# Cross attention: the maxima of two PSUM banks taken by one VectorE instruction, four banks for maxima and two for scores

## The chip, the cores and the metric

One core of one Trainium2 chip runs the whole program. The metric is device microseconds of one execution; lower is better. The kernel before was timed in three runs, and one more execution was taken with the hardware profiler.

## The reference

The kernel computes one decoder layer over x of 8 batches x 256 rows x 128 features: a causal self attention, a cross attention, and a rotary attention with 31 routed experts. The change is in the cross attention alone, for each batch b:

```
q = layernorm(x) @ Wq + bq                   # 256 x 128: 16 heads of 8 features
k, v = split(ctx_768 @ Wkv + bkv)            # 1601 x 128 each, contraction over 96
attn = softmax(q k^T / sqrt(8))              # per head 256 queries x 1601 keys, no mask
x = x + (attn v) @ Wo + bo
```

The softmax has to take off each query's largest score before the exponential.

## The kernel before, in words

Five engines run their own instruction streams and meet at semaphores. The program is a sequence of blocks: self attention, cross attention (`cross_attention`, about 300 to 1090 us of the profile, its main part from 350 us on), rotary attention, gates and experts. Within the cross attention:

- **Operands.** Queries and keys are split in three bf16 parts, whose six products are stacked along the partitions (`q_stack`, `k_stack`, 48 of 64 rows of a half), so that one bf16 matmul gives an accurate fp32 score. SyncE bounces the parts through DRAM scratch tensors (`bounce`, L976) and reads them back stacked (`load_half`, L989; half 0 serves heads 0 to 7, half 1 heads 8 to 15).
- **Groups.** The 16 heads make 4 groups of `GH` = 4. `part(i, r, ...)` works on the 13 key tiles (`KT`) of group g = (r + 1) % 4, one **step** n per key tile. So a batch is 4 parts of 13 steps. The last part of a batch, group 0, is already the next batch's.
- **Scores of a step** (L1387). Two halves (`par` 0 and 1) of two heads each: 2 matmuls of 256 queries into one PSUM bank, then ScalarE takes the exponential of the 128x512 half (L1277) into `b_prob`. The halves rotate over three banks, (5, 6, 7).
- **Values** (`values`, L1351). Four fp32 matmuls (eight instructions in the profile) of `b_prob` with `b_v_aug`, each in its own 32 columns of the array, summed over 13 steps in bank 1. Those of step n - 1 are issued in step n, behind the scores of step n.
- **Maxima.** Before a group is started its 256x1601 scores have to be known once for their maxima. A **unit** (`unit`, L1342) is one matmul of 128 queries of one head against a quarter of the keys (`CHUNKS`, 400 or 401 columns), for which VectorE takes one maximum per row (L1142) into `b_chunk_max`. A group has `UNITS_B` = 2 x 4 x 4 = 32 units; they rotate over three banks, (2, 3, 4). `units_of_step` spreads them over the steps of the part before: steps 0 to 8 (`M_STEP` = 9) do the last 21 (`HEAD`) units of the next group, steps 9 to 12 the first 11 of the one after it, 2 or 3 in a step. After a group's last unit VectorE folds `b_chunk_max` into `b_mneg` (L1146).
- **Items** (`PREP_AT`, L823, and `item`). At most one in a step, all through bank 0 (`prep`), each waiting until the one before is out of it (`prep_free`). Per batch: four `k` (keys of the next batch: two fp32 matmuls on PE, L1304; two ScalarE copies, L1230 and L1231; a split on GpSimd), `x`, `q`, four `v`, four `m` (transposes of `b_mneg`, L1324, which become the shift rows of `q_stack` by four small DMAs, L999), four `pv` (normalisation of a group, L1329 and L1160 to L1161 on VectorE), `attnT` and `out`. `("k", 0)` stands at r = 0, n = 0, the other `k` at n = 3, 5, 7, `pv` at n = 2 of each part, `m` at n = 9 of each, `q` at r = 0, n = 11. At r = 0, n = 2 VectorE also scales the next batch's rows (`norm_scale`, L127), in front of that step's units.
- **Waits of PE.** Score half i waits for exponential i - 3 (three banks), unit v for maximum v - 3, the values of a step for that step's second exponential. The first unit of a half (r = 1 and r = 3, n = 9) waits for the reload of that half (`stacked`).

The order of a step on PE (`part`, L1373) is: both score halves; the first unit; the second; the item; the values of the step before; the third unit where there is one. The prologue takes all 32 maxima of group 0 and 11 of group 1 before the first step. In the last batch nothing is prepared for a next one, and from r = 1, n = 9 on there are no units either.

## Time and profile before

| | |
|---|---|
| median of 3 runs | 1765.2 us (1760.3 to 1766.73) |
| the profiled execution, its own time | 1764.87 us |
| its span in the profile | 1763.0 us |
| busy over the span | PE 1537.7, DVE 1124.7, ACT 918.5, POOL 557.0 us |
| granted TensorE clock, mean | 0.939 of 2.4 GHz |

A tile name is the program's without buffer numbers; L1142 is a line of the kernel before. PE is TensorE's matmul stream, PEld its weight loads, DVE VectorE, ACT ScalarE, POOL GpSimd, SPq the DMA queue of SyncE. A timeline row has the start (us from the span's start), the length, the engine, the line, the operation, how many instructions were merged in it, and in brackets how long the engine sat idle before it and what ended that. Matmuls overlap: their ends are modelled, and what a matmul costs its engine is the distance from its start to the next one's.

### The profile page before, as it was taken

The numbers are of one execution on the slowest core, as the hardware profiler recorded it, in microseconds if no ns is written. First come the engines' busy times: TensorE is split into PE (matmuls) and PEld (weight loads), VectorE is DVE, ScalarE is ACT, GpSimd is POOL, SyncE is SP. The second block draws the span as 40 slices with busy tenths as digits, with TensorE's granted clock in tenths as the row PEclk, the third lists the DMA queues.
The fourth block names the chain that finished last, engine by engine and source line by source line (L and its number), as shares of the span: only waits on it lengthen the run. The fifth ranks groups of instructions, "written<-read, shape, count | busy, mean of one in ns | idle before, by whom it ended". The sixth has DMA issues, their size and how long they took to land. (4 is left out here: it accounts for less than half of the span.)

```text
span 1763.0 us, 29632 instructions
## 1 busy us (share of the span) xinstructions
PE 1537.7 (87%) x10917; PEld 836.1 (47%) x10941; DVE 1124.7 (64%) x2537; ACT 918.5 (52%) x1996; POOL 557.0 (32%) x690
## 2 busy tenths in 40 slices
PE   1677686699999999999999997899999997599998
PEld 1344343244454544444444443666666675244443
DVE  4755443587878786878787882566665663355554
ACT  1223233076777767777767775455555553234333
POOL 4010102030211212030303000788887884133332
PEclk9988787599999999999999998999999997699999
DMA  4222211703232323232332300000000000000001
GB/s 103 68 56 55 55 37 42 132 19 81 48 99 48 99 48 99 48 99 48 91 56 72 55 7 9 1 1 2 1 1 1 1 1 1 10 20 20 23 20 36
DMA packets 76276, 75.32 MB, mean 43 GB/s; under 512 B 11813, under 2 KB 65477, under 8 KB 75205
## 3 DMA queue, kind: packets, MB, share of 16 engines
q1 hardware_dynamic: 76132, 73.44, 18.9%
q8 instruction: 87, 1.43, 0.3%
q14 instruction: 57, 0.46, 0.1%
HBM read 42.73 MB, written 30.42 MB: 41 GB/s over the span
## 5 line engine op out<-in xcount | busy, mean ns | idle before, releaser
L1142 DVE TENSOR_REDUCE b_chunk_max<-psum 128x1 f32<-128x400 f32 (+1 forms) x1024 | 540.5, 570 | 161.6 <-PE psum L1348 154.5
L1277 ACT ACTIVATE b_prob<-psum 128x512 f32<-128x512 f32 (+1 forms) x832 | 450.5, 594 | 182.1 <-PE psum L1387 176.2
L1348 PE MATMUL psum<-k_stack,q_stack 128*128 128x400 bf16 (+1 forms) x1024 | 286.5, 343 | 21.0 <-DMA k_stack<-b_k_scratch 16.8
L1357 PE MATMUL psum<-b_prob,b_v_aug 128*32 128x256 f32 (+1 forms) x3328 | 265.8, 391 | 1.7 <-ACT b_prob L1277 0.4
L1387 PE MATMUL psum<-q_stack,k_stack 128*128 128x256 bf16 (+1 forms) x1664 | 254.2, 275 | 3.7 <-ACT b_prob L1277 3.3
L1387 PEld LDWEIGHTS psum<-q_stack,k_stack 128*128 128x128 bf16 (+1 forms) x1664 | 145.6, 99 | 123.1 <-ACT b_prob L1277 74.6
L2025 DVE TENSOR_TENSOR e_hg<-e_gl,e_gate 128x512 f32<-128x512 f32 x128 | 125.0, 996 | 113.0 <-PE psum L2040 65.9
L1546 POOL TENSOR_SCALAR c_prob<-c_prob,c_rec 128x128 f32<-128x128 f32 (+1 forms) x256 | 192.5, 769 | 8.9 <-POOL c_kT L1555 8.3
L1629 DVE SCALAR_TENSOR_TENSOR c_turned<-psum,c_bias,c_tab 128x256 f32<-128x256 f32 x256 | 106.1, 476 | 111.9 <-PE psum L1762 111.9
L1664 ACT ACTIVATE c_prob<-psum,c_mneg 128x128 f32<-128x128 f32 (+1 forms) x256 | 104.3, 419 | 136.2 <-DVE c_mneg L1606 136.2
L1348 PEld LDWEIGHTS psum<-k_stack,q_stack 128*128 128x128 bf16 x1024 | 99.6, 98 | 131.9 <-DVE b_chunk_max L1142 97.4
L2006 ACT ACTIVATE e_gl<-psum,b1T 128x512 f32<-128x512 f32 x128 | 87.9, 687 | 140.9 <-PE psum L2053 134.7
L2040 PE MATMUL psum<-e_hg,e_w 128*128 128x512 f32 x256 | 132.3, 600 | 8.9 <-DVE e_hg L2025 8.9
L2053 PE MATMUL psum<-anT,e_w 128*128 128x512 f32 x256 | 133.5, 605 | 1.4 <-PEq L1811 1.4
L1762 PE MATMUL psum<-c_xT,c_w 128*128 128x256 f32 x512 | 129.1, 398 | 1.9 <-DVE c_turned L1629 1.5
L1991 POOL PARTITION_BROADCAST e_gate<-e_gate_row x32 | 73.7, 2306 | 175.9 <-DMA e_gate_row<-gates 141.4
L1357 PEld LDWEIGHTS psum<-b_prob,b_v_aug 128*32 128x32 f32 (+1 forms) x3328 | 65.6, 108 | 124.4 <-issue 94.0
L1076 POOL COPY b_v_aug<-b_v_new 128x768 f32<-128x768 f32 (+1 forms) x32 | 15.9, 529 | 320.7 <-issue 257.9
L1762 PEld LDWEIGHTS psum<-c_xT,c_w 128*128 128x128 f32 x512 | 97.9, 202 | 15.5 <-DVE c_turned L1629 2.6
L578 DVE TENSOR_REDUCE a_mneg<-psum 128x2 f32<-128x512 f32 (+1 forms) x96 | 65.3, 689 | 59.3 <-PE psum L752 58.1
L653 ACT ACTIVATE a_prob<-psum 128x1024 f32<-128x1024 f32 x64 | 51.8, 811 | 73.5 <-PE psum L723 72.4
L2040 PEld LDWEIGHTS psum<-e_hg,e_w 128*128 128x128 f32 x256 | 48.8, 192 | 71.9 <-issue 52.2
(210 smaller groups left out, 1929.4 us busy)
## 6 DMA issues: line engine op xcount, KB each, us to landing
k_stack<-b_k_scratch SPq DMA_DIRECT2D x32, 600.4 KB, 10.4
b_k_scratch<-b_kparts SPq DMA_DIRECT2D x7, 1200.8 KB, 4.4
b_k_scratch<-b_kparts SPq DMA_DIRECT2D x7, 800.5 KB, 6.1
b_ctxT<-in_ctx SPq DMA_DIRECT2D x8, 600.4 KB, 11.9
e_w<-in_L_ffn_re_w SPq DMA_DIRECT2D x62, 64.0 KB, 1.8
a_scratch<-a_parts SPq DMA_DIRECT2D x16, 192.0 KB, 2.2
k_stack<-a_scratch SPq DMA_DIRECT2D x16, 192.0 KB, 4.6
q_stack<-b_q_scratch SPq DMA_DIRECT2D x32, 96.0 KB, 2.2
```

What stands on the lines that cost most here:

```text
L1142: nc.vector.tensor_reduce(out=chunk_max[:, half, q, column4(hh), c:c + 1], in_=max_bank(v)[:, 0:w], axis=AX.X, op=ALU.max).then_inc(max_do ...
L1277: nc.scalar.activation(prob[0:k, buf, par * 2 * T:(par + 1) * 2 * T], st_bank(v, par)[0:k, :], ACT.Exp, scale=HD ** -0.5).then_inc(exp_don ...
L1348: nc.tensor.matmul(max_bank(T_.now("unit"))[:, 0:hi - lo], queries_of(qst, h, slice(q * P, q * P + P)), keys_of(kst, h, slice(lo, hi)), st ...
L1357: last = nc.tensor.matmul(pv[32 * hh:32 * hh + 32, :], v_aug[0:k, kt, g * GH + hh, :], prob[0:k, buf, c:c + T], start=(kt == 0), stop=(kt ...
L1387: lastmm = nc.tensor.matmul(st_bank(step, par)[0:k, (hh // 2) * T:(hh // 2) * T + T], keys_of(kst, h, slice(n * P, n * P + k)), queries_of ...
L1546: ins = nc.gpsimd.tensor_scalar(prob[:, w % PB, hh, lo:hi], prob[:, w % PB, hh, lo:hi], rec[:, w % PB, hh, q:q + 1], None, ALU.mult)
L1629: ins = nc.vector.scalar_tensor_tensor(out=turned[:, u % 2, m, w, :], in0=bank[:, w * T:(w + 1) * T], scalar=bias[:, m, w, u:u + 1], in1=t ...
L1664: ins = nc.scalar.activation(prob[:, u % PB, hh, lo:hi], psum[:, 2 + hh, lo:hi], ACT.Exp, bias=mneg[:, par, q, hh:hh + 1], accum_out=total ...
L1762: last = nc.tensor.matmul(bank[:, w * T:(w + 1) * T], weights[:, m, u * P:(u + 1) * P], xT[:], start=True, stop=True)
L2025: nc.vector.tensor_tensor(hg[:, k % BUFS, :], gl[:, k % BUFS, :], gate[j][:, c * TW:(c + 1) * TW], ALU.mult)\
L2040: nc.tensor.matmul(psum[:, c, :], w[:, j, 1, :], hg[:, buf, :], start=second.start, stop=False).then_inc(y_done, 1)
L2053: nc.tensor.matmul(psum[:, 4 + k % BUFS, :], w[:, j, 0, :], d["anT"][:, c * TW:(c + 1) * TW], start=True, stop=True)\
```

## The change

A unit becomes a **pair**: two matmuls of 401 columns (keys 0 and 400, or 800 and 1200; one key is taken twice) into two neighbouring banks, and one VectorE instruction that reduces both, 128x2 out of 128x802. Pairs alternate between banks 2, 3 and 4, 5. The scores keep banks 6 and 7, one for each half, so a half waits for its own exponential of the step before. A group has 16 pairs, of which `HEAD` = 11 fall to steps 0 to 8 (one each, two in steps 4 and 8) and 5 to steps 9 to 12 (two in step 12). The order of a step on PE becomes: first score half; a pair; second score half; values of the step before; the item; the second pair where there is one.

```diff
@@ -803,9 +803,11 @@
 KT = -(-SKV // P)
 CHUNKS = [(c * SKV // 4, (c + 1) * SKV // 4) for c in range(4)]
 CW = max(e - s for s, e in CHUNKS)
-UNITS_B = QT * GH * 4
+PAIRS, PW = 2, 401
+PAIR_STARTS = [(0, 400), (800, 1200)]
+UNITS_B = QT * GH * PAIRS
 M_STEP = 9
-HEAD = 21
+HEAD = 11
 
 
 def tile_rows(kt):
@@ -919,13 +921,15 @@
         k_scr = nc.dram_tensor("b_k_scratch", [P, NP, SKV], BF16, kind="Internal").ap()
         qst, kst, ident = t["qst"], t["kst"], t["ident"]
         prep, pv = psum[:, 0, :], psum[:, 1, 0:T]
-        MAX_BANKS, ST_BANKS = (2, 3, 4), (5, 6, 7)
-
-        def max_bank(n):
-            return psum[:, MAX_BANKS[(n - 1) % 3], :]
-
-        def st_bank(step, par):
-            return psum[:, ST_BANKS[(2 * (step - 1) + par) % 3], :]
+
+        def max_bank(n, k):
+            return psum[:, 2 + 2 * ((n - 1) % 2) + k, 0:PW]
+
+        def max_banks(n):
+            return psum[:, 2 + 2 * ((n - 1) % 2):4 + 2 * ((n - 1) % 2), 0:PW]
+
+        def st_bank(par):
+            return psum[:, 6 + par, :]
 
 
         w_loaded, ones_set, half_stacked = pre.w_loaded, sem("b_ones_set"), sem("b_half_stacked")
@@ -1135,11 +1139,10 @@
             def unit(u):
 
                 v = T_.up("unit")
-                q, c, hh = u // (4 * GH), u // GH % 4, u % GH
+                q, pair, hh = u // (PAIRS * GH), u // GH % PAIRS, u % GH
                 half = (T_.n["unit"] - 1) // UNITS_B % 2
-                w = CHUNKS[c][1] - CHUNKS[c][0]
                 dve.wait_ge(max_full, v)
-                nc.vector.tensor_reduce(out=chunk_max[:, half, q, column4(hh), c:c + 1], in_=max_bank(v)[:, 0:w],
+                nc.vector.tensor_reduce(out=chunk_max[:, half, q, column4(hh), 2 * pair:2 * pair + 2], in_=max_banks(v),
                                         axis=AX.X, op=ALU.max).then_inc(max_done, 1)
                 if u == UNITS_B - 1:
                     dve.wait_ge(max_done, T_.now("unit"))
@@ -1274,7 +1277,7 @@
                     k, buf = tile_rows(n), (v - 1) % 2
                     for par in range(2):
                         act.wait_ge(st_full, 2 * v - 1 + par)
-                        nc.scalar.activation(prob[0:k, buf, par * 2 * T:(par + 1) * 2 * T], st_bank(v, par)[0:k, :],
+                        nc.scalar.activation(prob[0:k, buf, par * 2 * T:(par + 1) * 2 * T], st_bank(par)[0:k, :],
                                              ACT.Exp, scale=HD ** -0.5).then_inc(exp_done, 1)
                     if n == 0 and not first:
                         T_.up("step", -1)
@@ -1341,12 +1344,13 @@
 
             def unit(g, u):
                 T_.up("unit")
-                wait(pe, max_done, T_.now("unit", 3))
-                q, c, hh = u // (4 * GH), u // GH % 4, u % GH
-                lo, hi = CHUNKS[c]
+                wait(pe, max_done, T_.now("unit", 2))
+                q, pair, hh = u // (PAIRS * GH), u // GH % PAIRS, u % GH
                 h = g * GH + hh
-                nc.tensor.matmul(max_bank(T_.now("unit"))[:, 0:hi - lo], queries_of(qst, h, slice(q * P, q * P + P)),
-                                 keys_of(kst, h, slice(lo, hi)), start=True, stop=True).then_inc(max_full, 1)
+                for k, lo in enumerate(PAIR_STARTS[pair]):
+                    last = nc.tensor.matmul(max_bank(T_.now("unit"), k), queries_of(qst, h, slice(q * P, q * P + P)),
+                                            keys_of(kst, h, slice(lo, lo + PW)), start=True, stop=True)
+                last.then_inc(max_full, 1)
 
             def values():
                 g, kt, buf, back = pending.pop()
@@ -1380,21 +1384,25 @@
 
                     step = T_.now("step")
                     k, buf = tile_rows(n), (step - 1) % 2
-                    for par in range(2):
-                        wait(pe, exp_done, 2 * step - 1 + par - 3)
+
+                    def scores(par):
+                        wait(pe, exp_done, 2 * step - 1 + par - 2)
                         for hh in (par, par + 2):
                             h = g * GH + hh
-                            lastmm = nc.tensor.matmul(st_bank(step, par)[0:k, (hh // 2) * T:(hh // 2) * T + T],
-                                                      keys_of(kst, h, slice(n * P, n * P + k)),
-                                                      queries_of(qst, h, slice(0, T)), start=True, stop=True)
-                        lastmm.then_inc(st_full, 1)
+                            last = nc.tensor.matmul(st_bank(par)[0:k, (hh // 2) * T:(hh // 2) * T + T],
+                                                    keys_of(kst, h, slice(n * P, n * P + k)),
+                                                    queries_of(qst, h, slice(0, T)), start=True, stop=True)
+                        last.then_inc(st_full, 1)
+
                     units = units_of_step(n) if units_left(r, n, last) else []
+                    unit_group = (g + 1) % 4 if n < M_STEP else (g + 2) % 4
+                    scores(0)
                     for u in units[:1]:
-                        unit_group = (g + 1) % 4 if n < M_STEP else (g + 2) % 4
                         if u == 0 and unit_group % 2 == 0:
 
                             pe.wait_ge(stacked, T_.up("stacked", 4 * 16))
                         unit(unit_group, u)
+                    scores(1)
                     if n == 1 and not first:
 
                         pe.wait_ge(pv_copied, T_.now("group", -1))
@@ -1404,15 +1412,13 @@
                     if n == 1 and r == 1:
 
                         pe.wait_ge(v_placed, T_.now("placed"))
-                    for u in units[1:2]:
-                        unit(unit_group, u)
+                    if pending:
+                        values()
+                    pending.append((g, n, buf, 1))
                     it = prep_item(r, n, first, last)
                     if it:
                         item(*it)
-                    if pending:
-                        values()
-                    pending.append((g, n, buf, 1))
-                    for u in units[2:]:
+                    for u in units[1:]:
                         unit(unit_group, u)
                 if r == 3 and not first:
                     T_.up("placed")
```

The first of two places on PE, where the wait for exponentials and for maxima stands: two steps in the middle of a part (n = 4 and the first half of n = 5, before). `q_stack,k_stack` are scores, `k_stack,q_stack` units, `b_prob,b_v_aug` values. Before:

```order
L1387 MATMUL psum<-q_stack,k_stack 128x256 x4
L1348 MATMUL psum<-k_stack,q_stack 128x400 x2
L1357 MATMUL psum<-b_prob,b_v_aug 32x256 x4
L1348 MATMUL psum<-k_stack,q_stack 128x400
L1387 MATMUL psum<-q_stack,k_stack 128x256 x4
```

Now:

```order
L1392 MATMUL psum<-q_stack,k_stack 128x256 x2
L1351 MATMUL psum<-k_stack,q_stack 128x401 x2
L1392 MATMUL psum<-q_stack,k_stack 128x256 x2
L1361 MATMUL psum<-b_prob,b_v_aug 32x256 x4
L1351 MATMUL psum<-k_stack,q_stack 128x401 x2
L1392 MATMUL psum<-q_stack,k_stack 128x256 x2
```

The second score half now has a pair between it and the first, and stands straight ahead of the values.

The second place on PE is an item: `("k", 2)` at r = 0, n = 5 with the step behind it (the rows of n = 6 stand below those of n = 5). `b_ctxT,b_wkv` is the item. Before:

```order
L1387 MATMUL psum<-q_stack,k_stack 128x256 x4
L1348 MATMUL psum<-k_stack,q_stack 128x400 x2
L1304 MATMUL psum<-b_ctxT,b_wkv 128x400
L1357 MATMUL psum<-b_prob,b_v_aug 32x256 x4
L1348 MATMUL psum<-k_stack,q_stack 128x400
L1387 MATMUL psum<-q_stack,k_stack 128x256 x4
```

Now:

```order
L1392 MATMUL psum<-q_stack,k_stack 128x256 x2
L1351 MATMUL psum<-k_stack,q_stack 128x401 x2
L1392 MATMUL psum<-q_stack,k_stack 128x256 x2
L1361 MATMUL psum<-b_prob,b_v_aug 32x256 x4
L1307 MATMUL psum<-b_ctxT,b_wkv 128x400
L1392 MATMUL psum<-q_stack,k_stack 128x256 x2
L1351 MATMUL psum<-k_stack,q_stack 128x401 x2
```

The item has moved from ahead of the values to behind them; the next step's first score half follows it at once.

## Rows read from the trace of the kernel before

**Rows 1.** Page, costliest groups: busy us, mean ns | idle before, releaser.

```profile
L1142 DVE TENSOR_REDUCE b_chunk_max<-psum 128x1 f32<-128x400 f32 (+1 forms) x1024 | 540.5, 570 | 161.6 <-PE psum L1348 154.5
L1277 ACT ACTIVATE b_prob<-psum 128x512 f32<-128x512 f32 (+1 forms) x832 | 450.5, 594 | 182.1 <-PE psum L1387 176.2
```

**Rows 2.** Windows, one batch long: PE, PEld, DVE, ACT, POOL busy, clock, DMA.

```profile
653.00:747.00 94.00, 89.71 (x809) 44.03 (x808) 73.97 (x155) 66.61 (x128) 17.24 (x22) 1.00 0.32 69
```

**Rows 3.** Timeline, PE alone, two steps up to an m item.

```profile
643.21 0.64 PE L1357 MATMUL psum<-b_prob,b_v_aug 128*32 128x256 f32 x8
643.78 0.61 PE L1387 MATMUL psum<-q_stack,k_stack 128*128 128x256 bf16 x4
644.23 0.50 PE L1348 MATMUL psum<-k_stack,q_stack 128*128 128x401 bf16 x2
644.66 0.64 PE L1357 MATMUL psum<-b_prob,b_v_aug 128*32 128x256 f32 x8
645.24 0.34 PE L1348 MATMUL psum<-k_stack,q_stack 128*128 128x401 bf16 x1
645.42 0.60 PE L1387 MATMUL psum<-q_stack,k_stack 128*128 128x256 bf16 x4
645.85 0.50 PE L1348 MATMUL psum<-k_stack,q_stack 128*128 128x400 bf16 x2
646.56 0.38 PE L1324 MATMUL psum<-ident,b_mneg 128*4 128x128 f32 x2 [0.20 <-DVE b_mneg L1146]
```

**Rows 4.** Timeline, PE and ACT, a k item and the exponential behind it.

```profile
656.74 0.39 PE L1387 MATMUL psum<-q_stack,k_stack 128*128 128x256 bf16 x2 [0.47 <-ACT b_prob L1277]
...
664.00 0.83 PE L1304 MATMUL psum<-b_ctxT,b_wkv 96*128 96x400 f32 x2
...
664.87 0.59 ACT L1230 ACTIVATE b_kf<-psum,b_bk 128x400 f32<-128x400 f32 x1
...
666.12 1.09 ACT L1277 ACTIVATE b_prob<-psum 128x512 f32<-128x512 f32 x2 [0.17 <-PE psum L1387]
```

**Rows 5.** Reductions at half clock (timeline), and groups of other shapes (by form).

```profile
328.13 15.50 DVE L1142 TENSOR_REDUCE b_chunk_max<-psum 128x1 f32<-128x400 f32 x32 [21.59 <-PE psum L1348]
...
L578 DVE TENSOR_REDUCE a_mneg<-psum 128x2 f32<-128x512 f32 x64 | 43.4, 689 | 20.7 <-PE psum L752 20.4
L653 ACT ACTIVATE a_prob<-psum 128x1024 f32<-128x1024 f32 x32 | 32.8, 1024 | 69.6 <-PE psum L723 69.6
```

**Rows 6.** Timeline, around k item 1, r = 0, n = 2 and 3.

```profile
656.22 1.99 DVE L127 TENSOR_SCALAR xn<-x_sb,mv,rstd 128x128 f32<-128x128 f32 x2
...
658.98 0.82 PE L1348 MATMUL psum<-k_stack,q_stack 128*128 128x400 bf16 x2
...
660.32 0.94 PE L1304 MATMUL psum<-b_ctxT,b_wkv 96*128 96x400 f32 x2 [0.51 <-DVE b_attn L1161]
```

**Rows 7.** From the q item to the reloaded keys: timeline; last line, the load's waiters.

```profile
675.36 0.59 PE L1311 MATMUL psum<-b_xT,b_wq 128*128 128x256 f32 x2
...
698.28 0.51 PE L1348 MATMUL psum<-k_stack,q_stack 128*128 128x400 bf16 x2 [1.62 <-DMA k_stack<-b_k_scratch]
...
  PE psum L1348: 5.5, 5
```

**Rows 8.** Timeline, PE, r = 3, n = 4.

```profile
732.39 0.34 PE L1348 MATMUL psum<-k_stack,q_stack 128*128 128x400 bf16 x1 [0.36 <-DVE b_chunk_max L1142]
```

**Rows 9.** Timeline, last batch: steps without units.

```profile
1072.54 11.11 ACT L1277 ACTIVATE b_prob<-psum 128x512 f32<-128x512 f32 x20 [0.24 <-PE psum L1387]
...
1079.27 0.64 PE L1357 MATMUL psum<-b_prob,b_v_aug 128*32 128x256 f32 x8
...
1080.38 0.64 PE L1357 MATMUL psum<-b_prob,b_v_aug 128*32 128x256 f32 x8
```

**Rows 10.** Weight loads: an item's by its line (ns min/median/max), the scores' by page.

```profile
L1304 PEld LDWEIGHTS psum<-b_ctxT,b_wkv x56: 186/190/193, 371.4 to 950.2; 96*128 96x128 f32 x56
...
L1387 PEld LDWEIGHTS psum<-q_stack,k_stack 128*128 128x128 bf16 (+1 forms) x1664 | 145.6, 99 | 123.1 <-ACT b_prob L1277 74.6
```

## Prediction, on record before the result

> **What bounds the kernel now.** I read the costliest groups first. VectorE's maxima are the largest group of all, 1024 instructions of 570 ns, and half of them are to vanish, so a reader may expect a large gain [rows 1]. The windows say otherwise: in a batch of 94 us PE is busy 89.7 us and VectorE 74.0, at the full clock of 2.4 GHz [rows 2]. PE's timeline shows how tight that is. Counting from start to start, a step with two units takes 1.45 us (643.21 to 644.66): values 0.57, scores 0.45, units 0.43. A third unit adds 0.18 (645.24 to 645.42), and no row but the last has a wait [rows 3]. So in ordinary steps PE is the bound, and VectorE's idle time ends with PE's next unit (154.5 of 161.6 us) [rows 1]. What can be gained are the places where PE waits, and what can be lost are new ones. The sum is therefore a list of places, per batch, seven batches with a full program and one without preparation.
>
> **What the change costs PE in ordinary steps: nothing.** The 32 units of 400 or 401 columns become 16 pairs of 2 x 401; scores and values keep their count; each step still goes into the values and out of them once. A step with one pair should take the same 1.45 us, one with two pairs 0.34 more.
>
> **VectorE.** A pair's reduction has no row. From 400 elements in 570 ns [rows 1] and 512 in 689 [rows 5] one element costs 1.06 ns, so 802 come to about 1.00 us, against 1.14 for two. That one instruction may run over two banks without a penalty is likely from ScalarE's, 1.02 us for 1024 elements over two banks against 0.59 for 512 [rows 1, 5]; the upper bound is two full instructions, 1.14. VectorE loses some 70 us of work over the kernel, and by itself that is worth nothing, since PE covers it; if PE did not, a pair of 1.0 us in a step of 1.45 would still fit. The Trainium skill, "VectorE: DVE Perf Modes", section on the trn2 errata, charges a fixed 120 cycles at 0.96 GHz for each instruction on PSUM, and advises fewer, larger ones. By that rule alone 512 x 0.125 = 64 us would go, were VectorE the bound; no wait above shows that it is.
>
> **Waits that go**, per batch:
> - k item 1. VectorE is held by the row scaling (1.99 us), so the second unit starts late and the item, which needs the `pv` item's bank, starts at 660.32 where 658.98 - 0.17 + 0.34 = 659.15 was due [rows 6]: 1.2 us. Now the item stands a values group later, and `pv` is normalised behind one pair instead of after three units. By my schedule from these durations 0.1 remains: gain 1.1.
> - m items. PE reaches the transposes at 645.85 + 0.34 = 646.19 and starts at 646.56 [rows 3]: 0.37 us. Now a values group lies before them, but the last pair ends later too; 0.1 remains. At r = 0 another wait covers it, at r = 1 the wait below decides: gain 0.37 + 0.25 + 0.25 = 0.9.
> - The second unit at r = 3, n = 4: idle 0.36 [rows 8], and since the next start was due 0.17 earlier than the modelled end, 0.5. Two banks' worth of slack removes it: gain 0.5.
>
> **Waits that come**, per batch:
> - Exponentials behind k items. ScalarE begins its copies 0.87 us after the item's matmul and is free for exponentials 1.25 later (664.00, 664.87, 666.12). Before, the step's values follow the item, so the copies overlap PE's work and no wait is shown [rows 4]. Now the item comes after the values. With M the start of its matmul, the first exponential of the next step starts at M + 2.12, ends 0.59 later [rows 1] and frees its bank at about M + 2.77. PE gets there at M + 0.68 (item) + 1.45 = M + 2.13. With three banks that score half could go; with two it waits: 0.64 us, or 0.3 where the step between has two pairs. k 2 costs 0.64, k 1 and k 3 stand before steps 4 and 8 and cost 0.3 each: loss 1.25. k 0 has its wait already, 0.47 idle and 0.17 of modelled end [rows 4]: 0.64 again, no change. Bounds: 0 if ScalarE gets its copies in earlier, 2.6 if each k cost 0.64.
> - The stretch from the q item to the first unit that needs the reloaded keys. ScalarE, GpSimd, two trips through DRAM: 698.28 - 675.36 = 22.9 us, and PE waits 1.62 at its end; five of seven batches wait, 5.5 us in all [rows 7]. PE's work cannot shorten this. But the change takes work out of it: a values group (0.57 and the 0.1 of going into it) and a unit (0.18) that stood behind q now stand before it, half a score group (0.2) moves behind the waiting pair, and two units (0.34) come in. So 0.7 us that used to be hidden has to be done outside: loss 0.7, and 0 for a batch whose chain is short. The waits of `v` items within it are gone too and give nothing.
> - Items' weights. After a values group PE's weight load and its first matmul start together, so the load is not hidden. An item's takes 190 ns, a score's 99 [rows 10]; the item now pays the larger. Where another wait covers it, this is nothing; for the six items x, three pv, attnT and out it is 0 to 0.5 us: I take 0.2. The Trainium skill, "TensorE: Matmul & The Clock Gate", section on architectural detail, says that PE's queue pulls weight loads ahead of matmuls in flight. By that rule this term is 0 and the total 1.4 us lower; the rows of the values show it only within one group.
>
> Sum: -1.1 - 0.9 - 0.5 + 1.25 + 0.7 + 0.2 = -0.35, times 7 = -2.5 us.
>
> **The last batch.** For 17 steps there are no units. A step takes 1.11 us (1079.27 to 1080.38), and ScalarE needs 11.11 / 20 x 2 = 1.11, both full [rows 9]. With two banks a loop closes: second score half, values and next first score half, 0.22 + 0.67; both exponentials, the first starting 0.49 behind its scores, the second 0.49 later, ending 0.59 after; the bank back after 0.06. That is 2.52 us for two steps, 1.26 each: 17 x 0.15 = +2.6. The m item in front of them moves back behind its values, so the shift rows come later, partly in the same time: I take +2.8 together. In full steps the same loop has 2.90 us to run in and does not bind.
>
> **The prologue.** At half clock 32 maxima take 15.5 us [rows 5]. A pair needs 0.67 us of PE before VectorE may begin, and with two pairs of banks that comes to about 0.965 us a pair: 15.5 again, begun 0.3 later. Of the part for group 1 one unit moves on. I take 0, between -1 and +0.5.
>
> Together -2.5 + 2.8 = +0.3 on the profiled 1764.87 us: 1765.2, which is also the median of the runs.
>
> **Rivals.**
> 1. *Slack absorbs the new waits: faster.* If ScalarE gets its k copies done without holding scores (those of k 0 too), 1.9 us a batch come back; if the chain from q follows the faster steps, 0.7 more. 7 x 2.6 = 18 us: 1747; with the first alone 1752. A third way to the same side is VectorE holding the steps with three units, of which a pair would relieve it: 3 x 0.57 = 1.71 us against 1.64 of PE. For it: ScalarE is busy only 66.6 of 94 us [rows 2]. Against: one wait of just the first kind exists already with three banks [rows 4], and 32 maxima in 15.5 us are 0.48 each [rows 5], so three fit in 1.45. The Trainium skill's advice in "VectorE: DVE Perf Modes", cited above, would favour this side. Chance 0.22.
> 2. *Two score banks bind in full steps: slower.* Place: second half of each step on PE, waiting for its exponential of the step before. In my schedule that has 0.37 us of slack, one way from half to half. It decides if scores to exponential and back take over 2.90 us for two steps instead of 2.52, say because ScalarE's start slips behind PE's pair. Beyond that, each 0.05 us costs 0.05 x 400 steps = 20 us: 1785. Milder, with k waits at their upper bound, the weight loads in full and 1.5 us from the chain, 7 x 2.4 = +17: 1782. Chance 0.16 for both.
> 3. *The instruction over two banks is slow.* At twice the time per element, 1.9 us a pair, VectorE needs 64 x 1.9 = 122 us a batch and becomes the bound: some 200 us more. Chance 0.02.
> 4. *It doesn't do what it says.* The order of instructions shows 16 reductions of two columns where 32 stood, so this is nearly excluded; it falls into no change.
>
> **How the numbers follow.** No change, within 0.5% (8.8 us, about what measurements of this kernel can tell): 0.60, forecast 1765. Its own range is 1757 to 1773. Rival 1 gives faster 0.22, rivals 2 and 3 slower 0.18. The range of 8 in 10 takes in rival 1 with its first term, 1751, and half of rival 2, 1778.
>
> **What would show it.** Maxima: 512 instructions of about 1.0 us, VectorE's busy time down by some 60 us. PE's one-pair steps 1.45 us from values to values. PE waiting for `b_prob` some 0.64 us two steps behind k 0 and k 2, and 0.3 behind k 1 and k 3; the 1.2 us at k 1 gone; the wait for the reloaded keys up to about 3 us in every batch; steps without units at about 1.26 us. The prediction is wrong if one-pair steps take over 1.5 us, if waits for `b_prob` stand in steps without a k item before them, or if the wait for the keys does not grow.

## The result and the profile after

The changed kernel took **1772.6 us** (median of 14 runs, 1767.5 to 1779.8) against 1763.7 for the kernel before (14 runs on the same chip, 1757.5 to 1766.7): ratio **1.006, 95% interval 1.0044 to 1.0075**. It is slower by 9 us in the medians and by 10 in the ratio; forecast was 1765, no change. The profiled execution took 1779.8 us (before: 1764.9), with a span of 1777.8. It is the slowest of the 14, so what it shows of the clock below is more than a typical execution has.

The page's groups that answer to [rows 1]:

```profile
L1145 DVE TENSOR_REDUCE b_chunk_max<-psum 128x2 f32<-128x802 f32 x512 | 500.9, 991 | 192.6 <-PE psum L1351 176.9
L1280 ACT ACTIVATE b_prob<-psum 128x512 f32<-128x512 f32 (+1 forms) x832 | 456.5, 596 | 164.3 <-PE psum L1392 153.2
```

The pair's reduction takes 991 ns (forecast 1.00 us). The kernel does what it says. VectorE's group is busy 40 us less (forecast some 60 to 70) and idles 31 us longer before its instructions.

Now PE's waits in the main part, 390 to 1060 us: releaser, total us, times, longest. Before:

```profile
PE psum L1348 <- DMA k_stack<-b_k_scratch: 5.5, 5, 1.6
PE psum L1324 <- DVE b_mneg L1146: 4.7, 23, 0.2
PE psum L1304 <- DVE b_attn L1161: 3.1, 6, 0.5
PE psum L1387 <- ACT b_prob L1277: 2.8, 6, 0.5
PE psum L1348 <- DVE b_chunk_max L1142: 2.5, 7, 0.4
PE psum L1315 <- DVE b_attn L1161: 1.8, 7, 0.3
PE psum L1315 <- ACTq L1255: 1.1, 7, 0.2
```

After:

```profile
PE psum L1351 <- DMA k_stack<-b_k_scratch: 13.9, 7, 2.8
PE psum L1392 <- ACT b_prob L1280: 7.5, 13, 0.6
PE psum L1392 <- PE psum L1318: 0.3, 2, 0.2
```

The four short waits on VectorE are gone, as forecast, and so is the one on ScalarE (L1315 is the v items). The wait for the reloaded keys rose from 5.5 to 13.9 us, in all seven batches. That for exponentials rose too. Its places are two steps behind the k items. In a batch's PE timeline, at the k items 0 and 1:

```profile
659.49 0.94 PE L1307 MATMUL psum<-b_ctxT,b_wkv 96*128 96x400 f32 x2
660.27 0.38 PE L1392 MATMUL psum<-q_stack,k_stack 128*128 128x256 bf16 x2
...
661.14 0.64 PE L1361 MATMUL psum<-b_prob,b_v_aug 128*32 128x256 f32 x8
662.37 0.39 PE L1392 MATMUL psum<-q_stack,k_stack 128*128 128x256 bf16 x2 [0.59 <-ACT b_prob L1280]
...
665.54 0.94 PE L1307 MATMUL psum<-b_ctxT,b_wkv 96*128 96x400 f32 x2
666.32 0.38 PE L1392 MATMUL psum<-q_stack,k_stack 128*128 128x256 bf16 x2
```

From the start of values to the start of the next scores is 0.57 us where nothing is waited for. Here 661.14 to 662.37 is 1.23, so this exponential costs 0.66 (forecast 0.64). The k item takes 0.78 from its start to the scores (665.54 to 666.32), where the forecast had 0.68. A step with one pair and no item, from values to values (649.18 to 650.63), takes 1.45 us as before:

```profile
649.18 0.64 PE L1361 MATMUL psum<-b_prob,b_v_aug 128*32 128x256 f32 x8
...
650.63 0.64 PE L1361 MATMUL psum<-b_prob,b_v_aug 128*32 128x256 f32 x8
```

**What was not foreseen** stands behind some of these waits. PE's timeline at one of them, and windows of the same stretch (PE, PEld, DVE, ACT, POOL busy, granted clock, DMA share, GB/s):

```profile
893.35 0.38 PE L1392 MATMUL psum<-q_stack,k_stack 128*128 128x256 bf16 x2
896.42 0.85 PE L1351 MATMUL psum<-k_stack,q_stack 128*128 128x401 bf16 x2 [2.70 <-DMA k_stack<-b_k_scratch]
897.07 0.64 PE L1392 MATMUL psum<-q_stack,k_stack 128*128 128x256 bf16 x2
897.63 1.08 PE L1361 MATMUL psum<-b_prob,b_v_aug 128*32 128x256 f32 x8
```

```profile
889.00:893.40 4.40, 4.40 (x44) 1.95 (x42) 3.26 (x4) 3.29 (x6) 0.00 (x0) 1.00 1.03 140
893.40:896.40 3.00, 0.33 (x3) 0.04 (x1) 1.18 (x2) 0.60 (x1) 0.00 (x0) 0.87 0.47 58
896.40:899.80 3.40, 3.38 (x18) 1.33 (x19) 1.12 (x2) 1.02 (x3) 0.00 (x0) 0.50 0.00 0
899.80:903.20 3.40, 3.40 (x26) 1.29 (x24) 1.66 (x3) 1.91 (x4) 0.00 (x0) 0.61 0.00 1
903.20:906.60 3.40, 3.40 (x38) 1.57 (x30) 2.69 (x4) 2.33 (x5) 0.00 (x0) 1.00 0.00 0
```

The granted clock falls from its upper level, 2.4 GHz, to 1.2, while PE still waits (0.87 in the second window), and is at 1.2 behind the wait (0.50 in the third). The values' eight instructions take 1.08 us instead of 0.64, and PE, fully busy, loses time in which no wait is shown. This happens in four of seven batches, behind waits of 2.27, 2.46, 1.75 and 2.70 us, but not behind the longest, 2.77. It happens once more behind the last batch's wait of 1.56 us for its shift rows. In the profile before it happens nowhere between 360 and 1080 us, where the longest wait for keys is 1.62.

**Why the keys wait grew.** The **chain** is the work whose end the wait waits for. It starts not at the q item but at the m item of r = 0, n = 9, behind whose shift rows SyncE issues the copies of the key and query parts and then the loads. In one batch of the changed kernel, the m item and SyncE's issues behind it:

```profile
678.54 0.38 PE L1327 MATMUL psum<-ident,b_mneg 128*4 128x128 f32 x2
```

```profile
679.81 2.36 SPq L1003 DMA_DIRECT2D q_stack<-b_mparts  x4
682.28 1.76 SPq L203 DMA_DIRECT2D b_k_scratch<-b_kparts  x3
685.89 3.10 SPq L203 DMA_DIRECT2D b_q_scratch<-b_qparts  x3
692.70 0.82 SPq L211 DMA_DIRECT2D q_stack<-b_q_scratch  x2
693.56 0.93 SPq L211 DMA_DIRECT2D k_stack<-b_k_scratch  x2
```

The keys' first unit follows at 704.65, 26.1 us behind the m item, of which PE waits 2.46. Over the batches that wait, this chain takes 24.5 to 26.4 us after, mean 25.6, and 25.0 to 26.4 before, mean 25.9. The kernel before has two batches in which the keys landed ahead of PE, 24.6 and 24.7 us behind the m item, and these are not in its mean. Taken to the landing of the keys in all seven batches the chain is 25.5 us before and 25.6 after: it has not changed. PE's own work in it, the chain less the wait, is the same to 0.01 us in every batch of a kernel: **24.81 us before, 23.64 after**. The change saves 1.17 us of PE's work inside the chain, and all of it comes back as waiting. That this work is equal in every batch would hold from the q item too and does not tell where the chain starts. The queue does: on average the first copy of key parts is issued 3.7 us behind the m item in either kernel, and `a_q_early` below rules the q item out.

**The difference of the two profiled executions, stretch by stretch.** Up to the first unit: +3.3 us. This start lies between 327.0 and 331.9 us over all kernels of this study, old order and new, so it is no part of the change. Prologue: +0.6. Six batches, k item 0 to k item 0: 573.2 against 563.9, +9.3. From the seventh k item 0 to the next block's first transpose: +3.1. The blocks behind it: -1.5. Together 14.8, of which 13.0 are in the changed part.

### The profile page after: what moved, and what is told of

It is laid out like the page before. It is cut to its first block and busy times, and to the rows that moved or that the text cites. A ratio compares the mean times of both kernels' runs of the same rounds, so it can differ in the third digit from the quotient of the medians.

```text
span 1777.8 us, 29120 instructions
## 1 busy us (share of the span) xinstructions
PE 1549.1 (87%) x10917; PEld 837.2 (47%) x10941; DVE 1088.8 (61%) x2025; ACT 923.3 (52%) x1996; POOL 555.8 (31%) x690
## 5 line engine op out<-in xcount | busy, mean ns | idle before, releaser
L1145 DVE TENSOR_REDUCE b_chunk_max<-psum 128x2 f32<-128x802 f32 x512 | 500.9, 991 | 192.6 <-PE psum L1351 176.9
L1280 ACT ACTIVATE b_prob<-psum 128x512 f32<-128x512 f32 (+1 forms) x832 | 456.5, 596 | 164.3 <-PE psum L1392 153.2
L1392 PE MATMUL psum<-q_stack,k_stack 128*128 128x256 bf16 (+1 forms) x1664 | 321.7, 276 | 13.8 <-ACT b_prob L1280 8.7
L1351 PE MATMUL psum<-k_stack,q_stack 128*128 128x401 bf16 x1024 | 268.7, 345 | 30.6 <-DMA k_stack<-b_k_scratch 27.1
L1351 PEld LDWEIGHTS psum<-k_stack,q_stack 128*128 128x128 bf16 x1024 | 92.6, 99 | 87.4 <-issue 32.5
```

The lines of the kernel that those rows point to most:

```text
L1145: nc.vector.tensor_reduce(out=chunk_max[:, half, q, column4(hh), 2 * pair:2 * pair + 2], in_=max_banks(v), axis=AX.X, op=ALU.max).then_inc ...
L1280: nc.scalar.activation(prob[0:k, buf, par * 2 * T:(par + 1) * 2 * T], st_bank(par)[0:k, :], ACT.Exp, scale=HD ** -0.5).then_inc(exp_done, 1)
L1351: last = nc.tensor.matmul(max_bank(T_.now("unit"), k), queries_of(qst, h, slice(q * P, q * P + P)), keys_of(kst, h, slice(lo, lo + PW)), s ...
L1392: last = nc.tensor.matmul(st_bank(par)[0:k, (hh // 2) * T:(hh // 2) * T + T], keys_of(kst, h, slice(n * P, n * P + k)), queries_of(qst, h, ...
```

## Experiments

Each ran beside the kernel before on its chip, and ratios are to it. A "batch" is from one k item 0 to the next in the profiled execution, mean of six; before: 93.98 us.

**The changed kernel again.**

> The changed kernel once more, beside the others of this set. Both theories: 1772 us, +8 on the kernel before. It gives the reference for the three others on the same chip, and a second profile: by the chain theory the waits for the reloaded keys (r = 1, n = 9) sum to 12 to 16 us over seven batches, and the granted clock is at half behind the longest of them (over 1.8 us) and not behind the short ones.

1776.1 us, 1.0076 (1.0055 to 1.0097). Keys wait 13.9 us in 7, the same to a tenth; but half clock behind two of them instead of four, and none behind the shift rows. The two are waits of 1.97 and 2.22 us, while the clock stayed full behind 2.88, 2.53 and 2.25, so the expectation of half clock behind the longest waits missed. Batches of 94.85 us. The sum of the waits repeats and the clock does not.

**Where the item stands.** b_item_last: the kernel before with the item moved behind the values, the rest untouched; a_item_first: the changed kernel with it moved back.

```
-                    it = prep_item(r, n, first, last)
-                    if it:
-                        item(*it)
                     if pending:
                         values()
                     pending.append((g, n, buf, 1))
+                    it = prep_item(r, n, first, last)
+                    if it:
+                        item(*it)
```

> Kernel before with one part of the change alone: the item behind the values. m waits (1.1 us a batch) and most of the 1.2 us at k item 1 go; waits behind k items come for the second score half (0.35 each), weights cost 0.1 an item, and the keys wait grows by some 1.5 us with the half clock behind it where it passes 2 us: 1762 + 5 = 1767 us. If the half clock did not exist or the position was harmless: 1761.

> Changed kernel with the item put back ahead of the values, pairs and banks as changed. By the schedule of the prediction: waits for exponentials behind k items (1.94 us a batch) go, item weights are hidden again (0.1 each), one values group returns into the stretch of the chain (keys waits 0.67 shorter, less half clock); against that m items wait 0.55 more at three places and k item 1 0.6 more: 1774 - 10 = 1764 us. If the position of the item is harmless: 1774.

b_item_last 1769.2 us, 1.0046 (1.0027 to 1.0065), as expected. Its waits:

```profile
PE psum L1348 <- DMA k_stack<-b_k_scratch: 14.0, 7, 3.0
PE psum L1387 <- ACT b_prob L1277: 3.5, 12, 0.5
PE psum L1348 <- DVE b_chunk_max L1142: 2.5, 7, 0.4
```

and the clock is at half behind four of the seven keys waits and behind the shift rows. Moving the item alone gives the whole of the keys wait, 14.0 us, and a loss that can't be told from the full change's (1.0046 against 1.006 and 1.0076, intervals overlapping), without pairs, banks or score halves being touched. a_item_first 1770.3 us, 1.0051 (1.0033 to 1.0069), 6 us worse than expected:

```profile
PE psum L1327 <- DVE b_mneg L1149: 13.6, 22, 0.6
PE psum L1351 <- DMA k_stack<-b_k_scratch: 8.4, 7, 2.1
PE psum L1392 <- ACT b_prob L1280: 4.7, 6, 0.8
```

The keys wait falls by 5.5 us, but the m item now stands right behind the last pair, whose reduction takes 0.99 us and not 0.57, and waits 0.6 each time. By these times alone the two places of the item can't be told apart as long as the chain binds; `ac_item_first` below tells them apart without it.

**The clock.** Six transposes whose result nobody reads, on PE just ahead of the keys wait at r = 1.

```
+                            wait(pe, max_done, T_.now("unit", 1))
+                            for k in range(6 if r == 1 else 0):
+                                nc.tensor.transpose(psum[:, 2 + 2 * (T_.now("unit") % 2), 0:P], ident[:], ident[:])
```

> Changed kernel with six dummy transposes (fp32, 128 columns, 1.3 us in all) on PE just ahead of the wait for the keys at r = 1, into the bank that the next pair overwrites; the chain is untouched. If the half clock behind the long waits is a cost of its own: idle gaps shrink from up to 2.9 to 1.6 us, the clock stays at 2.4 GHz in the cross attention's batches, and 5 us come back, 1767. If the clock falls anyway or costs nothing: 1772 to 1774, since in the batches with the shortest waits (1.05 and 1.2 us) the dummies are just covered.

1770.2 us, 1.0044 (1.0028 to 1.006): 6 us below the changed kernel on the same chip (the means are 5.5 apart, uncertain by some 3), by useless work. The clock stays at 1.00 in all seven batches, behind waits up to 2.24 us:

```profile
791.88 0.82 PE L1405 MATMUL psum<-ident 128*128 128x128 f32 x6
794.94 0.52 PE L1351 MATMUL psum<-k_stack,q_stack 128*128 128x401 bf16 x2 [2.24 <-DMA k_stack<-b_k_scratch]
```

At the last batch's shift rows no transposes were put; there, in the same execution, the clock falls to half behind a wait of 1.69. This is one profiled execution, and without transposes the falls come and go, so the median of seven runs carries the argument more than the profile does.

**Which end of the chain binds.** The forecast had the q item. a_q_early and b_q_early move it, in either kernel:

```
-           (0, 10): ("x", 0), (0, 11): ("q", 0),
+           (0, 4): ("x", 0), (0, 6): ("q", 0),
```

> Changed kernel with the items x and q at r = 0, n = 4 and 6 instead of 10 and 11, so that the chain from q over two trips through DRAM to the reloaded keys begins some 7 us earlier. Chain theory (the loss is the wait for the keys, 15.0 us in the profiled execution, and the half clock behind it, 6.5 us): both go, 1772 - 19 = 1753 us, no half clock between 357 and 1075 us. Rival (the loss is the new order itself: waits for exponentials behind k items, 1.94 us a batch, and item weights not hidden, 0.1 each): only 1 or 2 us change, 1770.

> The same move of x and q in the kernel before. Chain theory: its keys wait of 6.4 us over seven batches goes, its clock never fell there: 1764 - 6 = 1758 us, so the change itself would be a gain of 4 to 5 us once the chain is out of the way. Rival: 1763, and the changed kernel stays 8 slower with q early too.

Both missed, by 30 and 10 us: 1782.7 us, 1.011 (1.0092 to 1.0129), and 1767.6, 1.003 (1.0015 to 1.0046). Keys wait 18.9 and 8.9 us, longer than unmoved; the clock is at half behind all seven in a_q_early, behind one in b_q_early. The reason is the account from above, with m item to keys as the chain:

| kernel | chain, mean of the batches that wait | PE's own work in it | keys wait |
|---|---|---|---|
| before | 25.9 | 24.81 | 5.5 in 5 |
| b_q_early | 25.4 | 24.16 | 8.9 in 7 |
| b_item_last | 25.8 | 23.81 | 14.0 in 7 |
| a_item_first | 25.4 | 24.23 | 8.4 in 7 |
| after | 25.6 | 23.64 | 13.9 in 7 |
| a_q_early | 25.6 | 22.87 | 18.9 in 7 |

Two items less of PE's work in it, the chain as long as before, and after the change the wait is longer by what they took (0.72 us a batch for 0.77 of work). Computing the query parts earlier does not help: in a_q_early their copies are issued 5.6 us behind the m item instead of 7.3, and land 13.3 behind it instead of 13.5, because in the queue they stand behind the key parts' copies, which land at 11.8 in both. What hangs on the m item is the copy of the key parts, 2.4 MB, issued behind the shift rows' store. The next kernels cut it in the quarters in which GpSimd delivers it, and issue three ahead of that store:

```
             def bounce():
-                wait(sp, stacked, T_.now("stacked"))
-                sp.sem_inc(passed, 1)
-                sp.wait_ge(k_split, T_.up("kchunk", 4))
-                bounce_parts(sp, k_scr, kparts[:], 1, k_bounced)
+                bounce_chunks(3, 4)
...
+                if r == 0 and not last:
+                    wait(sp, stacked, T_.now("stacked"))
+                    sp.sem_inc(passed, 1)
+                    bounce_chunks(0, 3)
                 if prep_item(r, M_STEP, first, last):
                     store_m(PREP_AT[(r, M_STEP)][1])
```

a_chunks and b_chunks have this edit alone, a_chunks_q and b_chunks_q the early x and q items too.

> Changed kernel, x and q early as before, and the key parts bounced in quarters: three of them in SyncE's queue ahead of the shift rows' store, the last quarter behind it. Revised chain theory: with q early the chain begins with the bounce of all key parts (2.4 MB), which stands behind the shift rows' store in SyncE's queue; with three quarters gone before, the reload starts at the end of part r = 0 and lands 11 us later, before r = 1, n = 9. The keys wait (about 15 us) and the half clock behind it (4 to 6) go: 1774 - 20 = 1754 us. Rival (order itself is the loss): 1772 or above.

> The same in the kernel before. Revised chain theory: its keys wait of 6.4 us goes: 1762 - 6 = 1756 us, so that the change itself is then worth -2 us (between -6 and +2). Rival: 1760, the change still +10.

> Changed kernel, key parts bounced in quarters, x and q where they were. Tells which end of the chain binds. If the chain from q binds too (q is projected at n = 11, its own split, bounce and the reload follow): keys waits stay at 1 us or more a batch, 1768 us. If only the large bounce behind the shift rows' store binds: the waits go and it comes to 1750 without moving q.

> The kernel before with the key parts' copies cut in quarters, three of them ahead of the shift rows' store, and nothing else: the clean partner of a_chunks (ratio 0.9958, batches of 92.13 us). Theory 'the order itself is worth 1.05 us a batch, and the change lost by the chain of the keys alone': keys wait below 0.5 us in all seven batches, clock at full through the main part, batches of 93.2 us (93.98 less 0.8 of keys wait), last batch as before (153.7); 1757.5 us, ratio 0.997, so that the change is worth -2 us with the chain out of the way. Rival 'the keys wait costs the kernel before more than the trace shows': 1753 us, ratio 0.994, and the change would be worth nothing.

| kernel | us | ratio (interval) | keys wait | batch |
|---|---|---|---|---|
| b_chunks | 1758.6 | 0.9972 (0.9959 to 0.9985) | 0 | 93.2 |
| a_chunks | 1755.8 | 0.9958 (0.994 to 0.9976) | 0 | 92.1 |
| b_chunks_q | 1757.1 | 0.9979 (0.9963 to 0.9995) | 0 | 93.2 |
| a_chunks_q | 1747.6 | 0.9925 (0.9902 to 0.9948) | 0 | 91.4 |

SyncE's queue in a_chunks. The m item is at 669.92; the first row is two of the three quarters that go ahead, the third row the last quarter; the loads of the keys are issued 11.0 us behind the m item instead of 15.0:

```profile
662.16 5.71 SPq L203 DMA_DIRECT2D b_k_scratch<-b_kparts  x6
671.19 2.40 SPq L1005 DMA_DIRECT2D q_stack<-b_mparts  x4
673.63 1.65 SPq L203 DMA_DIRECT2D b_k_scratch<-b_kparts  x3
...
680.90 0.93 SPq L211 DMA_DIRECT2D k_stack<-b_k_scratch  x2
```

b_chunks and b_chunks_q came 1 us above what was expected; a_chunks lies between its two expectations (1750 and 1768) and nearer the first, and a_chunks_q is 6 us below its own.

With the chain out of the way the order is worth what the sum had: batches of 92.1 instead of 93.2 us, and over the whole kernel the ratio of a_chunks to b_chunks is 0.9986, uncertain by some 0.2%, so that the gain is shown by the profiles' batches and not by the times. With x and q also moved it is 0.7 us more a batch (a_chunks_q), and the kernel is faster than before by 0.75%.

**The terms of the order**, each on a_chunks_q as the base. ac_two_reduces takes a pair's maxima by two instructions of one bank; ac_item_first puts the item back ahead of the values; ac_mixed does so for x, q, v, attnT, out and half of pv; ac_units puts the two extra pairs of the first nine steps in steps 0 and 7 instead of 4 and 8.

```
-                nc.vector.tensor_reduce(out=chunk_max[..., 2 * pair:2 * pair + 2], in_=max_banks(v), ...)
+                for k in range(2):
+                    ins = nc.vector.tensor_reduce(out=chunk_max[..., 2 * pair + k:2 * pair + k + 1], in_=max_bank(v, k), ...)
```

```
-        lo, k = UNITS_B - head, M_STEP
-        return [lo + u for u in range(n * head // k, (n + 1) * head // k)]
+        lo, ends = UNITS_B - head, (0, 2, 3, 4, 5, 6, 7, 8, 10, 11)
+        return [lo + u for u in range(ends[n], ends[n + 1])]
```

> From here on the base is the changed kernel with x and q early and key parts bounced in quarters (1747.6 us). This one undoes the change's title: each pair is reduced by two instructions of one bank each (1024 of 570 ns again), order, pairs and banks as changed. By the prediction VectorE's saved time lies wholly beside PE: 1748 us, at most 3 more from m items, which wait 0.1 longer each. If the saved time on VectorE is where the gain of 10 us over the same base of the kernel before comes from: 1756.

> The new base with every item ahead of the values again. Gains: k waits of 1.0 us a batch and unhidden weights of 16 x 0.1; losses: m items 0.55 more at four places, k item 1 0.6, v item 3 0.4. Sum +0.6 a batch: 1752 us. If the item's new place is only a cost (with the chain out of the way too): 1740.

> The new base with x, q, v, attnT, out and the pv items of r = 2 and 3 ahead of the values (their weight loads are hidden there), k, m and the other two pv behind. By the schedule no wait comes back, and eleven weight loads of 0.1 us a batch are hidden: 1747.6 - 7 = 1741 us. If the weight loads cost nothing behind the values: 1748.

> The kernel with the change, quarters and early items, with the two extra pairs of the first nine steps in steps 0 and 7 instead of 4 and 8. Theory 'an exponential that stands behind a k item costs 0.3 us more where the step has one pair than where it has two': the wait behind k item 0 falls from 0.66 to 0.3, that behind k item 3 from 0.33 to 0, the batch from 91.42 to 90.8, 4 us on seven batches: 1743.5 us, ratio 0.990. Rival 'the wait only moves to the steps that lost a pair': within 1 us of 1747.6, ratio 0.9925.

- ac_two_reduces: 1753.9 us, 0.9935 (0.9909 to 0.9961), batches of 91.6 us against 91.4. **The instruction over two banks, which the change is named for, is worth some 0.2 us a batch in this order**, all of it in the steps with m items, though it takes 991 ns for what two do in 2 x 569. The times of the whole kernels differ by less than their noise.
- ac_item_first: 1767.9 us, 1.0029 (1.0014 to 1.0044), batches of 93.9; a miss by 16 us. The m item waits 18.0 us in 29 and the exponentials 4.7. This is the largest term: with pairs and the chain out of the way, the item behind its values makes a batch 2.5 us shorter. Without that move the pairs and banks lose: 93.9 against 93.2 in b_chunks_q.
- ac_mixed: 1755.2 us, 0.9949 (0.9932 to 0.9966), batches of 92.3; expected 1741. The weights' 0.05 to 0.1 us an item were won and more was lost: x and q now wait for ScalarE to empty the bank that all items share, in six batches each, and a v item waits likewise, 1.7 us in seven:

```profile
PE psum L1316 <- ACTq L1241: 2.6, 6, 0.4
PE psum L1319 <- ACTq L1241: 2.6, 6, 0.4
```

- ac_units: 1754.6 us, 0.9947 (0.9928 to 0.9966); expected 1743.5. The wait for exponentials behind k item 0, 0.66, is gone, and in the step of k item 0 a wait of the second pair for maxima has come, 0.37 (0.22 of it idle). The expectation had 0.3 left, as a wait for exponentials. The batch still rose from 91.4 to 92.2, because k item 1 again waits for the normalisation, the wait of [rows 6]:

```profile
655.46 0.94 PE L1312 MATMUL psum<-b_ctxT,b_wkv 96*128 96x400 f32 x2 [0.70 <-DVE b_attn L1169]
```

**The last batch.** Steps without pairs go in twos of 2.52 us in the changed kernel (1088.47 to 1090.99), forecast 2.52:

```profile
1088.47 0.88 PE L1392 MATMUL psum<-q_stack,k_stack 128*128 128x256 bf16 x4
...
1090.99 0.88 PE L1392 MATMUL psum<-q_stack,k_stack 128*128 128x256 bf16 x4
```

ac_last_banks lets these steps' scores take turns over four banks (two of the maxima's are free there), ac_last_banks2 the same from the second such step on; ac_best is ac_last_banks with the pairs of ac_units; ac_again is a_chunks_q once more.

```
+        def st_bank(par, spare=False):
+            return psum[:, (2 if spare else 6) + par, :]
+
+        def spare_of(r, n, last):
+            return not units_left(r, n, last) and (r * KT + n - KT - M_STEP) % 2 == 0
...
-                        wait(pe, exp_done, 2 * step - 1 + par - 2)
+                            wait(pe, exp_done, 2 * step - 1 + par - 4)
```

> The same base, and in the last batch's seventeen steps without pairs the scores take turns over four banks (two of the maxima's, free there, beside their own two). Theory 'the pitch of 1.26 us a step there is the loop scores, exponential, scores over two banks': two steps fall from 2.52 to 2.2 us, the last batch from its start to the last store by 2.6 us: 1745 us, ratio 0.991. Rival 'the pitch there is ScalarE with two exponentials and their gaps': steps stay at 1.26 and the time at 1747.6.

> Both of the two edits on the same base: the sum of the two, 4 + 2.6 us off 1747.6: 1741 us, ratio 0.988, if each is as expected and they do not touch; 1745 us if only the last batch's loop goes.

> The kernel of a_chunks_q once more, to stand beside the next one on one chip: 1747 to 1752 us, ratio 0.990 to 0.995, batches of 91.42 us, steps without pairs at 1.26 us.

> The same as ac_last_banks, with the two spare banks taken by the second step without pairs rather than the first, whose scores had waited 1.09 us for the last pair's maxima. Theory 'the loop's gain was spent on that wait': the wait goes, steps stay at 1.12 us, and from the last m item to the transpose of the result 21.3 + 5.6 us become 25 or less; 2 us below ac_again, ratio 0.991. Rival 'the shift rows' round trip ends last there in any case': their wait grows by what the loop gives, with the clock at half behind it, and the time is ac_again's within 1 us.

ac_last_banks 1749.9 us, 0.9916 (0.9895 to 0.9937); ac_best 1750.7, 0.9922 (0.9901 to 0.9942), where 1741 was expected; ac_again 1747.9, 0.9925 (0.9908 to 0.9943); ac_last_banks2 1748.9, 0.9929 (0.991 to 0.9948). The pitch is the loop over two banks: with four it is 1.11 to 1.12 us a step. But nothing comes of it. In ac_last_banks2:

```profile
1052.04 0.64 PE L1369 MATMUL psum<-b_prob,b_v_aug 128*32 128x256 f32 x8
1054.47 0.61 PE L1405 MATMUL psum<-q_stack,k_stack 128*128 128x256 bf16 x4 [1.80 <-DMA q_stack<-b_mparts]
1055.01 1.07 PE L1369 MATMUL psum<-b_prob,b_v_aug 65*32 65x256 f32 x8
```

From the m item to the scores that need its shift rows is 5.42 us, against 5.46 in ac_again: the round trip ends last, its wait is 1.80 instead of 1.51, and the clock is at half behind it where it stayed at full in ac_again. From the seventh k item 0 to the last group's transpose ac_last_banks2 takes 151.5 us and ac_again 151.7. The rival was right, and the two cannot be told apart in time.

## Why the prediction was wrong, point by point

- **Number and direction.** 1772.6 us lies inside the range of 8 in 10 and, by a hair, inside the range of the no-change forecast, 1757 to 1773. That is no merit: the kernel moved by +0.6%, clear of zero, where nothing was to happen, and from the middle forecast it is 8 us away.
- **Order, seven batches: the sum right, in part by luck.** The sum without the chain, -1.1 - 0.9 - 0.5 + 1.25 + 0.2, was -1.05 us a batch; b_chunks to a_chunks, 93.2 to 92.1, it is -1.1. The terms, read from the length of the steps with each item beyond a plain step (1.45 us, and 0.17 for each unit beyond two), five batches:

| term, us a batch | forecast | b_chunks to a_chunks |
|---|---|---|
| k items, with the wait at k 1 | -1.1 | -0.9 |
| m items | -0.9 | -1.2 |
| the unit at r = 3, n = 4 | -0.5 | -0.5 |
| v items | 0 | -0.5 |
| exponentials behind k items | +1.25 | +1.5 |
| weights of the other items | +0.2 | +0.4 |

The wait behind k 0, 0.63 in b_chunks, stands there in a pv step and is taken off in the fifth row. The four waits for exponentials are 0.66, 0.31, 0.66 and 0.31 (forecast 0.64 and 0.3). The waits of the v items, set down as giving nothing, and the m items gave more than forecast; the weights of the k items, set down nowhere, and the other weights took it back. VectorE's relief was forecast at nothing and is worth next to nothing.
- **"The stretch from the q item to the first unit that needs the reloaded keys": the step that failed, twice.** First the size: +0.7 us a batch was written, and it is (13.9 - 5.5) / 7 = +1.2. From the q item to the keys PE does 1.03 us less (21.30 before, 20.27 after), not 0.7: the waits of the v items, 0.41 us in each batch, were part of PE's time there, so removing them did not "give nothing" but lengthened the wait. And the chain was put at the q item; it hangs on the m item before it, from where PE does 1.17 us less (24.81, 23.64). Every such microsecond is waited for in full.
- Second, and larger: **the wait was priced without what comes behind it.** The text took [rows 2]'s full clock for granted; the half clock is a term that it put at nothing. In the profiled execution four stretches at half clock cost 1.6, 1.5, 1.6 and 2.75 us (the batch's length, less 92.1 and its keys wait), some 7.4 together; in a_again two of them, 3.1. Eight more microseconds of waiting brought three to seven of slow running. a_dummy, which takes only this away, gives 6 us back. Over the 14 runs the mean granted clock goes with the time: 0.943 in the fastest (1767.5 us), 0.928 in the slowest (1779.8).
- **The last batch, +2.8: the mechanism right, the size open by the clock.** From the m item on it is +0.8 for the shift rows and +1.5 for the loop where the clock stays at full (ac_two_reduces: 19.9 us from the shift rows to the last transpose, before 18.4), so +2.3; with half clock behind the shift rows another 1.2 (21.1 us in the changed kernel).
- **Added up.** Order -6.5 (seven batches without keys wait and half clock, 92.14 against 93.07 us), keys wait +8.4, half clock +3.1 to +7.4, last batch +2.3 to +3.5, prologue +0.6: +7.9 to +13.4 us, an estimate from these rows. The profiled execution has 13.0, the runs 9 to 10.
- **Weights.** Behind its values an item of type k, v, q or out costs 0.1 us more (a k item lengthens its step by 0.77 instead of 0.67), one of type x, pv or attnT 0.05. The weight loads of a k item, before and after:

```profile
663.83 0.36 PEld L1304 LDWEIGHTS psum<-b_ctxT,b_wkv 96*128 96x128 f32 x2
```

```profile
669.87 0.30 PEld L1307 LDWEIGHTS psum<-b_ctxT,b_wkv 96*128 96x128 f32 x2 [0.41 <-issue]
669.87 0.94 PE L1307 MATMUL psum<-b_ctxT,b_wkv 96*128 96x400 f32 x2
```

Before, the load starts 0.17 us ahead of its matmul (664.00, [rows 4]); after, behind the values, both start at 669.87. The Trainium skill, "TensorE: Matmul & The Clock Gate", section on architectural detail, says that weight loads can be pulled ahead of matmuls in flight. The trace agrees for the load behind units; where the item's 128-wide load follows values in 32 columns of the array it does not happen here.
- **Prologue:** +0.6 us for 0, just past the upper bound (+0.5).
- **Rivals.** No full step is bound by two score banks (1.45 us), the reduction is not slow, slack does not absorb the new waits. The loss came by none of the rivals alone; the nearest was the milder form of rival 2, which counted 1.5 us from the chain but no clock. Together with rival 3 the slower side had 0.18. Its chance should have been higher: the keys wait was already in five of seven batches, and every term that gained ran into it.

Order of worth of the parts, as far as shown: the item behind its values gains 2.5 us a batch with pairs and the chain out of the way, and brings the keys wait with the chain in the way; the joined instruction gains 0.2 at most. How much of the rest is due to the score half between the maxima was not tried apart.

## What to carry to other kernels

When PE is the bound and a transfer ends a few of its waits, find what that transfer's chain hangs on and take PE's own work between there and the wait (the time less the wait). To find that start look at the queue: what stands in it ahead of the transfer, and what its first issue follows. Work saved there comes back as a wait; only a shorter chain turns it into a gain. Here the change alone was +0.6%, and with the copy of the key parts in quarters ahead of a store, and two items earlier, -0.75%, on two chips. Price a long wait of PE with the stretch behind it, and read the granted clock there in several executions, since it does not come every time.

## What the runs showed of the hardware

- Behind waits of 1.5 to 3.3 us the granted clock was at half in some executions and at full in others: behind 2.88 us at full (a_again), behind 1.75 at half (after); the same batch's wait of 2.5 us was followed by half clock in after (704.65) and by full in a_again (703.67). Behind the keys wait a stretch cost 1.5 to 1.6 us, and 2.75 in the one batch in which the clock stayed low for longer. The Trainium skill, "TensorE: Matmul & The Clock Gate", section on HAM oscillation, tells of a kernel with half clock behind every one of its DMA waits; in this case only a_q_early, with waits of 2.1 to 3.3 us, shows that.
- One reduction over two banks takes 991 ns for 802 elements, one of 401 takes 569: 147 ns saved by joining two. The group's busy time fell by only 40 us (540.5 to 500.9) where 512 x 0.147 = 75, because reductions right behind each other overlap: the prologue's 32 single ones took 15.5 us in [rows 5], 0.48 each. Over the whole kernel count times mean is 583 us before against 540.5 busy, and 507 after against 500.9.
